# A transformer layer with eight routed experts: output projection in three passes, token lists without pad rows behind their counts

## The reference

```python
def layer(x, ctx):                     # x (2, 1024, 256), ctx (2, 77, 256)
    q = heads(layernorm(x) @ w_q.T);  k = heads(ctx @ w_k.T);  v = heads(ctx @ w_v.T)
    a = softmax(q @ k.T * 16 ** -0.5) @ v
    x = x + merged(a) @ w_o.T
    z = layernorm(x)
    scores = sigmoid(z @ gate_w.T)
    sel = top_k(scores + expert_bias, 2)          # the two experts of a token
    shared = (silu(z @ sw1.T) * (z @ sw3.T)) @ sw2.T
    for each token and each selected e, with s = scores[e]:
        r = s * z
        out += s * ((silu(r @ w1[e].T) * (r @ w3[e].T)) @ w2[e].T)
    return x + shared + out
```

## Time and profile before

| what | value |
|---|---|
| times of three runs, us | 295.43, 300.84, 296.78 (median 296.78) |
| profiled execution, us | 295.51, span 293.7 |
| mean granted TensorE clock | 0.988 |
| busy: PE, DVE, ACT, POOL, us | 278.0, 185.9, 165.6, 143.8 |
| DMA | 35.37 MB, mean 120 GB/s |

### The profile page before, as it was taken

The page is one execution under the profiler, slowest core; times in us unless marked ns, Lnnn a source line. Parts: engine busy times, 40 slices in busy tenths (PEclk is TensorE's granted clock), DMA queues, the critical chain, the costliest instruction groups (busy, mean ns, idle before and its releaser), DMA issues.

```text
span 293.7 us, 6561 instructions
## 1 busy us (share of the span) xinstructions
PE 278.0 (95%) x1989; PEld 244.7 (83%) x1989; DVE 185.9 (63%) x700; ACT 165.6 (56%) x404; POOL 143.8 (49%) x234
## 2 busy tenths in 40 slices
PE   7689999999999999999985999999999999999966
PEld 7478889988988999987764898888888998888855
DVE  1648555556765778776874466666766666653675
ACT  2147787778867655556432355665666555554421
POOL 8004776666698837765660013333333333333390
PEclk9999999999999999999998699999999999999999
DMA  7269633343341112211282213333333333211796
GB/s 234 26 158 405 224 102 105 107 108 95 95 138 56 37 39 74 75 55 59 73 234 63 72 54 112 108 98 106 111 110 107 98 107 111 90 44 49 261 390 226
DMA packets 23996, 35.37 MB, mean 120 GB/s; under 512 B 8123, under 2 KB 14907, under 8 KB 23835
## 3 DMA queue, kind: packets, MB, share of 16 engines
q1 hardware_dynamic: 17072, 24.43, 27.1%
q0 software_dynamic: 3408, 9.41, 9.1%
q10 hardware_dynamic: 3483, 1.11, 1.6%
HBM read 22.07 MB, written 12.87 MB: 119 GB/s over the span
## 4 chain that ended last, share of the span: by engine, by line
PE 86%; DMA 4%; DVE 3%; POOL 2%; issue 2%; ACT 1%; SPq 0%; DVEq 0%; POOLq 0%
PE psum L986 15%; PE psum L987 13%; PE psum L988 13%; PE psum L1056 13%; PE psum L992 9%; PE psum L1010 6%; PE psum L1045 5%; PE psum L1072 5%; POOL lists L415 2%; PE psum L1039 2%; DMA lists<-rows,dest 2%; PE psum L1090 1%; DMA value_rows<-hid 1%; PE psum L1125 1%; DMA v_rows<-value_rows 1%
## 5 line engine op out<-in xcount | busy, mean ns | idle before, releaser
L451 POOL DMA_INDIRECT results<-probs_t,place x39 | 37.2, 955 | 81.0 <-ACT probs_t L558 81.0
L1056 PEld LDWEIGHTS psum<-vals,probs_t 128*128 128x128 f32 x320 | 37.9, 192 | 3.2 <-issue 2.6
L1056 PE MATMUL psum<-vals,probs_t 128*128 128x51 f32 x320 | 39.9, 274 | 0.3 <-DVE vals L626 0.3
L424 POOL TENSOR_TENSOR w_lo<-w_stage,w_hi 128x256 fp32r<-128x256 f32 x54 | 37.8, 730 | 4.5 <-ACT w_hi L499 4.5
L415 POOL DMA_INDIRECT lists<-rows,dest x32 | 31.7, 990 | 16.5 <-DVE dest L761 9.3
L543 ACT ACTIVATE act_s<-psum,share 128x256 f32<-128x256 f32 x39 | 18.5, 475 | 32.3 <-PE psum L988 32.3
L986 PE MATMUL psum<-w_lo,x_hi 128*128 (+1 forms) x82 | 36.2, 441 | 0.0
L800 DVE TENSOR_REDUCE row_max<-psum 128x16 f32<-128x1232 f32 x16 | 23.0, 1438 | 20.5 <-PE psum L988 20.4
L854 DVE TENSOR_TENSOR h_lo<-psum,h_hi 128x256 fp32r<-128x256 f32 x55 | 23.3, 423 | 20.1 <-ACT h_hi L474 20.1
L986 PE MATMUL psum<-w_lo,h_hi 128*128 (+1 forms) x110 | 31.8, 289 | 3.3 <-DVE h_lo L854 3.3
L988 PE MATMUL psum<-w_hi,x_hi 128*128 (+1 forms) x82 | 32.4, 395 | 0.0
(11 more groups left out here) (169 smaller groups left out, 677.1 us busy)
## 6 DMA issues: line engine op xcount, KB each, us to landing
w_stage<-in_ffn SPq DMA_DIRECT2D x27, 256.0 KB, 2.8
probs<-lists SPq DMA_DIRECT2D x39, 131.0 KB, 2.1
w_hi<-results SPq DMA_DIRECT2D x7, 512.0 KB, 6.7
out_x<-resid SPq DMA_DIRECT2D x7, 256.0 KB, 2.9
lists<-pad_rows SPq DMA_DIRECT2D x9, 131.0 KB
resid<-in_x SPq DMA_DIRECT2D x1, 1024.0 KB, 10.2
x_t<-in_xt SPq DMA_DIRECT2D x1, 896.0 KB, 8.4
x_t<-in_xt SPq DMA_DIRECT2D x1, 768.0 KB, 5.4
```

What stands on the lines that cost most here:

```text
L424: pool.tensor_tensor(w_lo[:, to], w_stage[:, of], w_hi[:, to].bitcast(F32), ALU.subtract).then_inc(s["split_lo"], 1)
L451: pool.indirect_dma_start(results, bass.IndirectOffsetOnAxis(ap=place[:, j:j + 1], axis=0), y_rows[:, cols(par)], None).then_inc(b_out[par ...
L1056: last = mm(o_b[:, head_base(c) * HV:(head_base(c) + VHEADS) * HV], probs_t[:, cols(c, P)], vals[:, cols(batch * CHUNKS + c, VHEADS * HV)] ...
```

## The change

There are four parts.

1. **Output projection in three passes.** `wo` is split once, at the start, into `wo_hi` (ACT) and `wo_lo` (POOL). It is loaded ahead of the wait for the value rows, into the buffer that `wq` had, once `wq` has been centred. The attended rows are divided into `x_t` (the inputs of that tile are no longer needed), transposed, copied by ACT to `h_hi`, and DVE's new `attended_low` makes `h_lo`. `projected` issues six fp32r matmuls. `attn_transposed` and its copy move ahead in the turn, and ACT's third weight part moves to the end of the turn.
2. **Lists without pads behind the counts.** SP writes pads to the first 128 rows of all eight regions, and to the region of unused tiles, amid the weight loads; POOL's first scatter waits for them. An expert's last tile no longer starts at a multiple of 128 but so far back that it ends with the last row (`limit`); rows that it has in common with the tile before get no expert (`NO_EXPERT`) and a dump row (`no_place`). The table on DVE has 18 steps instead of 11.
3. **Spreading product two items later**: behind `step_b(4)`, on PE and DVE; it now spreads two numbers a tile.
4. **Half a shared tile ahead of the ranks**: the first three products of `gate_up(0)` stand ahead of the ranks of tiles 10 and 11.

Some small buffers share space with others now (`th`, `score` and their like in `v_rows0`, `mean_of` in `hid`). The diff, cut to what works:

```diff
-TABLE_LINKS = 11
+TABLE_LINKS, ROW_LINK = 18, 16
+SPREAD_WITH = 4
+PADS_WITH = 3 * STAGES
...
+            sp.wait_ge(s["centred"], 1)
+            sp.dma_start(wo, wot).then_inc(s["wo_in"], 16)
             sp.wait_ge(s["v_stored"], 16)
...
-            sp.dma_start(wo[:, :], wot).then_inc(s["wo_in"], 16)
...
+                if n == PADS_WITH:
+                    sp.wait_ge(s["pads_done"], 4)
+                    first_rows = lists[0:EXPERTS * REGION, :].rearrange("(e r) c -> r e c", e=EXPERTS)[0:P]
+                    sp.dma_start(first_rows, pad_rows[:, :].unsqueeze(1)
+                                 .to_broadcast([P, EXPERTS, ROW])).then_inc(s["pad_out"], 16)
+                    sp.dma_start(lists[EXPERTS * REGION:, :], pad_rows[:, :]).then_inc(s["pad_out"], 16)
...
-            sp.wait_ge(s["counted"], 1)
-            _, n_rows = nc.values_load_multi_w_load_instructions(counts_i[0:1, :], engines=(mybir.EngineType.SP,))
-            for e in range(EXPERTS):
-                sp.dma_start(lists[bass.ds(n_rows[e] + e * REGION, P), :], pad_rows[:, :]).then_inc(s["pad_out"], 16)
-            sp.wait_ge(s["table_step"], TABLE_LINKS)
-            sp.wait_ge(s["pad_out"], 16 * (EXPERTS + 1))
+            sp.wait_ge(s["table_step"], ROW_LINK)
...
+                if t == 0:
+                    pool.wait_ge(s["pad_out"], 32)
...
             query_scale(0)
+            pool.wait_ge(s["wo_high"], 1)
+            for kt in range(KT):
+                pool.tensor_tensor(wo_lo[:, cols(kt)], wo[:, cols(kt)], wo_hi[:, cols(kt)].bitcast(F32),
+                                   ALU.subtract).then_inc(s["wo_low"], 1)
...
+            act.wait_ge(s["wo_in"], 16)
+            act.activation(wo_hi[:, :], wo, ACT.Copy).then_inc(s["wo_high"], 1)
...
                 peaks(i)
-                high_parts(parts_at(i)[2:])
                 exponentials(i, 0)
                 exponentials(i, 1)
...
-                if live(i - 4):
+                if i == TILES - 1:
                     logits(i - 4)
                 if live(i - 1):
-                    copied(attn_t[:, :], a_b[:, 0:DIM], "at_ps", i, "at_out")
+                    copied(h_hi[:, :], a_b[:, 0:DIM], "at_ps", i, "at_out")
+                if live(i - 4) and i < TILES - 1:
+                    logits(i - 4)
                 probs_out(i, 0)
                 probs_out(i, 1)
                 probs_out(i, 2)
+                high_parts(parts_at(i)[2:])
...
+            def attended_low(t):
+                dve.wait_ge(s["at_out"], t + 1)
+                tt(h_lo[:, :], a_b[:, 0:DIM], h_hi[:, :].bitcast(F32), ALU.subtract).then_inc(s["at_low"], 1)
...
+                if i == 1:
+                    values(1)
                 if live(i + 1):
                     query_low(i + 1)
+                if live(i - 1):
+                    attended_low(i - 1)
...
             divided(TILES - 1)
+            attended_low(TILES - 1)
             route_choice(before_last)
...
-            for n in range(4, ITEMS):
+            for n in range(SPREAD_WITH + 1, ITEMS):
...
             def projected(t):
-                pe.wait_ge(s["at_out"], t + 1)
+                pe.wait_ge(s["at_low"], t + 1)
                 for kt in range(KT):
-                    last = mm(a_b[:, 0:DIM], attn_t[:, cols(kt, P)], wo[:, cols(kt)],
-                              start=kt == 0, stop=kt == KT - 1)
+                    last = product(a_b[:, 0:DIM], [v[:, cols(kt, P)] for v in (h_hi, h_lo)],
+                                   [v[:, cols(kt)] for v in (wo_hi, wo_lo)], start=kt == 0, stop=kt == KT - 1)
...
             pe.wait_ge(s["split_lo"], SHARED_PARTS * (PART // PIECE))
+            gate_up(0, shared, range(0, 1))
             ranks(len(GROUPS) - 3)
...
-            gate_up(0, shared)
+            gate_up(0, shared, range(1, KT))
             normed_transposed(TILES - 2)
...
             down(2, shared)
-            experts_spread()
             for n in range(3, ITEMS):
                 step_b(n)
+                if n == SPREAD_WITH:
+                    experts_spread()
```

More of the change, by code:

```diff
@@ L225, in layer_kernel @@
     probs, probs_t = sb("probs", PCOLS), sb("probs_t", PCOLS)
-    th, score, ranked, top8 = (sb(n, 4 * EXPERTS) for n in ("th", "score", "ranked", "top8"))
+    th, score, ranked, top8 = (v_rows0[:, cols(n, 4 * EXPERTS)] for n in range(4))
     top8_i = sb("top8_i", 4 * EXPERTS, U32)
@@ L259, in layer_kernel @@
     y_rows = probs_t[:, 0:2 * DIM]
+    expert_f, twice, no_place = (probs_t[:, 2 * DIM + n * TILES_B:2 * DIM + (n + 1) * TILES_B] for n in range(3))
     sum_tiles = w_hi[:, 0:TILES * TOPK * DIM].bitcast(F32).rearrange("p (t w) -> p t w", t=TILES)
@@ L821, in _ @@
                     keys(1)
-                    values(1)
                 g = group_ending(i - PLACES)
@@ L931, in _ @@
             placed_last(last)
+            ts(spare[:, :], n_rows, float(-P), 0.0, ALU.add, ALU.max).then_inc(table, 1)
             h_low(1)
@@ L956, in _ @@
             shared_added(2)
-            step_b(3)
+            for n in range(3, SPREAD_WITH + 1):
+                step_b(n)
             dve.wait_ge(s["expert_ps"], 1)
-            dve.tensor_copy(expert_f[:, :], r_b[:, COUNT_COL:COUNT_COL + TILES_B]).then_inc(s["expert_ps"], 1)
+            ts(twice[:, :], r_b[:, COUNT_COL + TILES_B:COUNT_COL + 2 * TILES_B], float(P), first_row[:, :],
+               ALU.mult, ALU.is_gt).then_inc(s["expert_ps"], 1)
+            dve.wait_ge(s["expert_ps"], 2)
+            stt(expert_f[:, :], twice[:, :], NO_EXPERT, r_b[:, COUNT_COL:COUNT_COL + TILES_B],
+                ALU.mult, ALU.add).then_inc(s["expert_ps"], 1)
+            dve.wait_ge(s["dumps"], 1)
+            tt(no_place[:, :], twice[:, :], dump[:, 0:TILES_B], ALU.mult).then_inc(s["expert_ps"], 1)
             def summed(g):
@@ L1155, in _ @@
                     queries(i + 1)
-                if live(i - 4):
+                if i == TILES - 1:
+                    gates(i - 4)
+                if live(i - 1):
+                    attn_transposed(i - 1)
+                if live(i - 4) and i < TILES - 1:
                     gates(i - 4)
```

82 lines of the change are left out of this document (48 added, 34 removed).

## The result

The changed kernel takes **301.4 us** in the median of 20 runs (297.22 to 305.27), the kernel before 299.59 in the median of 20 beside them. The ratio is **1.0078, 95% interval 1.0043 to 1.0113**: 0.8% slower, where 2.6% faster had been forecast. The profile shown here is of a run that took 302.25.

The account below looks back on a forecast made before the run. TensorE was taken to bound attention, GpSimd's scatters the change of phase. Terms -2.4, +0.7 and -2.2 make -3.9; with -2.8 for the clock, -6.7 from 295.51 gives 288.8, plus 0.2 is 289.0 us; range 286.8 to 292.2.

Parts of the forecast that it names:

- Projection in three passes: Attention loop: six fp32r products replace four-pass fp32 ones, gaining 0.15 to 0.16 a tile over 15 tiles, -2.4 us.
- What must cover it: Attention loop: the new copy and subtraction end 0.15 us before PE wants them in tile 11, so no cost was taken.
- rival 2: Attention loop: the projection waits for `attended_low`, eating the 0.16 a tile; 291.4 us, chance 0.12.
- nobody waits for its 0.64 us in either place: Attention loop: moving ACT's third weight part, 0.64 us, to the end of the tile costs nothing.
- Tail: Tail of attention: added subtractions delay the ranks that release the last eight scatters by 0.7 us; half tile buys nothing.
- Pad rows: End of attention: without the late pads the last scatter lands in 2.6 us instead of 4.84, -2.2 us.
- Rival 4: Change of phase: pads gone but the slow scatter landing stays; 293.8 us with a fallen clock, 291.0 without; chance 0.08.
- the 1.8 of the prediction's other sum: Last scatter's landing: the pads' gain by the Trainium skill's HBM access times, 1.8 us instead of 2.2.
- Table: Change of phase, on DVE: the longer table ends 0.75 us later; net +0.4 for PE's last shared item.
- The sum: Change of phase: first list lands 3.9 us earlier, and a shorter PE idle avoids the low clock's 2.8; together -6.7 us.
- PE idle of about a microsecond or less: Change of phase: sign of a right forecast, PE's idle before the first list shrinking from 3.23 to about 0.6 us.
- Rival 1: Change of phase: the clock falls all the same, so only 3.9 us is gained; 291.6 us, chance 0.09.

Follow-up runs that it names:

- e6: Whole change, with VectorE's h_lo subtraction and ACT's h_hi copy moved ahead of the query's in the loop: median 297.97 us, ratio to the kernel before 0.9914.
- e14: Kernel of e11 (four passes, no subtraction), with ACT's rounding of the expert weights back at its old place: median 296.93 us, ratio to before 0.9977.
- e13: Kernel of e11 (four passes, no subtraction), with the attention transposes and ACT's copy back at their old place: median 298.99 us, ratio to before 1.0019.
- e10: The kernel of e6 (whole change, subtraction first) run once more, no further edit: median 297.19 us, ratio to before 0.9952.
- e11: Whole change in its order, but the projection as one four-pass float32 product, without split weights or subtraction: median 300.49 us, ratio to before 1.0134.
- e4: Whole change without the half shared tile ahead of the ranks: median 301.86 us, ratio to the kernel before 1.0055.
- e2: Only the list part (no late pads, longer table, later spreading product) on the kernel before: median 297.33 us, ratio 0.9931.
- e5: The kernel before, unchanged, run again for a second profile: that profiled run took 300.18 us, span 298.4.
- e3: Only the three-pass projection with its reordered loop on the kernel before, lists as before: median 306.64 us, no ratio because its runs scatter.
- e9: Kernel of e3 (projection alone) with the h_lo subtraction ahead of the query's: median 301.15 us, ratio to before 1.0084.
- e15: The list part alone on the kernel before, as in e2, run once more: median 297.75 us, ratio 0.9993.
- e16: Whole change with the subtraction first and ACT's weight rounding back at its old place, second time: median 299.04 us, ratio to before 1.0019.

## Why the prediction was wrong

The forecast of 289.0 misses the mean of 301.45 by 12.4. Of that 3.8 is the base: it starts from a run of 295.51 (and adds 0.2), where the mean of the kernel before is 299.5. The other 8.6 is the change, +1.9 instead of -6.7. The steps below divide it: projection and tail gave +3.9 where -1.7 was forecast, and the lists with the clock gave -1.9 where -5.0 was.

- *Projection in three passes, -2.4.* The size for a tile was right (0.16). The first step that failed, and the larger one, is "What must cover it", which took nothing for all 15 tiles from one tile's slack. By the experiments the subtraction's place costs 3.1 and the moves on PE and ACT 2.9 (1.2 of these 6.0 in rows of the loop). Tiles 2 and 3 have no gates product in front of the projection, and there PE waits for `h_lo` (0.5, gone in e6): rival 2, but in the tiles that I hadn't looked at. And "nobody waits for its 0.64 us in either place", said of the weight part on ACT, was wrong for a third engine: POOL's subtraction follows the rounding, and DVE is held by it (0.6 in tile 8; gone in e14, where the rounding is back, and not in e13, where it isn't). The three passes themselves are about as forecast: -2.2 (e6 and e10 against e11). Left of 1.7 for tiles 2 to 12: 0.14.
- *Tail, +0.7.* In size about right. In tile 15 the ranks come 7.22 after `row_max` (132.54 to 139.76), before 6.61 (126.78 to 133.39): +0.6, forecast +0.65. The half tile buys nothing (e4).
- *Pad rows, -2.2.* Right in size: 6.1 to 4.15 in the changed kernel, 3.5 in e2. Rival 4 is out. The reason given, a scatter that lands late because the pads share its DMA engines, fits the first profile alone; in e5, e3 and e9 it is the landing of the pads themselves that the read waits for. The 2.0 measured doesn't tell the 2.2 from the 1.8 of the prediction's other sum.
- *Table, +0.75.* From scan to last step it takes 2.28 (159.85 to 162.13) instead of 1.62, +0.66. It doesn't hold PE; PE's late signal does.
- *The sum, -3.9 and -2.8.* This is the second step that failed. It took the idle of 3.23 and the clock's fall behind it for properties of the kernel. They were read in one execution, 295.51 where the mean of 113 runs is 299.5. In the second profile (e5, 300.18) PE is behind by its late signals, reaches the list at 166.4 when it has lain there for some 2.8 (161.60 + 2.0), and so an earlier list is worth little: 1.9 for the whole part (e2, e15), part of it clock. The phase change does keep its clock in the changed kernel. But mean clock is 0.973, before 0.977: the low stretches stand in tiles 12 to 15 and the tail. "PE idle of about a microsecond or less" was wrong too: 2.45, for `h_lo`.
- *Rivals.* Rival 1 was nearest (the clock falls all the same), with its place wrong. Its 291.6 rests on the same good execution. Rival 2 names a wait that is there, but as a loss of 0.5 in two tiles and not of 0.16 in each.

The way from the kernel before to the whole change, in means: lists -1.9; the subtraction behind `q_lo` instead of ahead +3.1; the moved transposes and rounding, with the half tile and the earlier load of `wo`, +2.9 (e11 against the lists); three passes for four about -2.2 (e6 and e10 against e11). Together +1.9. The four are steps between measured kernels, so their sum is right by construction; each has an error of 0.4 to 0.8, and kernels taken at different times are compared. The rows in the loop show 0.6 of the second and 0.6 of the third. For the rest, small lateness of PE in tiles 12 to 15 and then half clock is an argument and not shown; the profile of e13, late and yet at whole clock, speaks against its being that simple. Two things stay open: what makes PE's signals late at 114 to 123 and past 150 (it is in both kernels, hence not of the change), and whether and why the granted clock answers to steps that move PE by tenths. A rival for the first, that PE waits for its code, is not tested. The profile names DMA queues "instruction". Near 115 and 120 each of the eighteen profiles has a packet of theirs, that of the first one too, which has no late signal; and in e5 they have none from 143 to 160.5, where PE is latest. So the traces don't speak for it.

No version tried is clearly better than the lists alone: 297.6 in the mean, against 299.5 of before and 301.5 of the whole change. Only e14, four passes with the rounding at its old place, is at 297.4, which is the same within the errors, for more changed code.

## What to carry to other kernels

Before a wait of one profile is put into a sum, see whether that execution is a usual one: its time against the spread of many runs, and a second profile, say more than any row in it. Slack must be read in the tile that has least cover, not in a steady one, and for a moved step also on the engine that is released by it. A gain of tenths a tile on a bound engine can be smaller than what the granted clock differs by from run to run (0.959 to 0.994 in the kernel before), so it takes many runs of both kernels, best beside each other, to see it at all.

## What the runs showed of the hardware

- Each 0.01 of mean granted clock goes with 2.2 us of 300. Low stretches were 3.4 or 6.8 long, and many lie behind stretches in which PE did less: 7.69 of 9.5 in e16 ahead of 122.5, 10.21 of 11.0 after 112.0 in the changed kernel, 16.89 of 20.5 in e5 ahead of 156.4. In the first profile of the kernel before, PE worked all 11 us from 112 to 123, and kept its clock there. But in e13 it worked 10.43 of those 11 us and 15.65 of the 20 from 143 to 163, and kept its clock too.
- A VectorE copy or SCALAR_TENSOR_TENSOR on 8 columns takes 0.65 instead of 0.17 beside a GpSimd subtraction of 0.73, and ends with it. A reduction of 64 columns beside the same subtraction takes 0.22, as elsewhere.
- With eight writes of 131 KB (the pads) from SyncE's queue at the end of the scatters, the first list read came 5.9 to 6.9 behind the last scatter (four profiles); without them 3.5 to 5.2 (fourteen).
- PE's signal to another engine came 1 to 4.6 us behind the product's record at some places of all profiles but one; another engine usually starts 0.3 behind it (ACT at 115.81 in e5, on a product recorded until 115.53).
